# Loading image 0 once: 32 partitions first, and a gate on four 32x32 pieces of the array

## The reference

```
# layer 0
g  = relu(bn2(wg1 @ x)).mean over pixels          # 32 gates; only image 0's are used
xg = relu(tanh(wg2 @ g + bg2)) + beta             # of image 0
p  = round(xg[0:31] / sum(xg) * 96)               # assigns DCT bases to channels
y  = sum over the 7x7 cells of (cell means of x) * filt   # filt from p
x  = x * relu(bn1(w1d @ y + b1d)) + x
# layer 1
t  = relu(bn(w1 @ mean of x));  wt = w2 @ t + b2  # a 3x3 depthwise kernel per image and channel
out = depthwise conv of x with wt, masked to 4 taps, + bias
```

## Time and profile before

| what | value |
|---|---|
| time, three runs | 214.06, 214.72 (median) and 216.6 us |
| profiled execution | 213.82 us, of which the span of its instructions is 211.8 us |
| HBM | 40.51 MB read, 38.54 MB written |
| TensorE, DVE, ACT, POOL busy | 88%, 79%, 76%, 61% of the span |

### The profile page before, as it was taken

The page is one execution under the profiler, slowest core; times in us unless marked ns, Lnnn a source line. Parts: engine busy times, 40 slices in busy tenths (PEclk is TensorE's granted clock), DMA queues, the critical chain, the costliest instruction groups (busy, mean ns, idle before and its releaser), DMA issues.

```text
span 211.8 us, 4505 instructions
## 1 busy us (share of the span) xinstructions
PE 186.0 (88%) x1678; PEld 106.1 (50%) x1678; DVE 167.5 (79%) x265; ACT 161.1 (76%) x310; POOL 128.9 (61%) x120
## 2 busy tenths in 40 slices
PE   7899999799889988998899889989998989988860
PEld 3458656446445544564455546444644544554430
DVE  3338789997898689878987898798969896877780
ACT  2020027878997899789979898889888997899970
POOL 0233049999999989886997699769779110310000
PEclk9999999999999999999999999999999999999997
DMA  5999999999999999999999999999999646535777
GB/s 149 361 426 429 425 426 426 425 310 402 433 420 422 432 423 424 432 426 422 431 429 416 429 412 418 426 429 422 435 417 429 280 204 265 223 161 227 308 303 303
DMA packets 8534, 79.34 MB, mean 375 GB/s; under 512 B 1056, under 2 KB 1696, under 8 KB 2496
## 3 DMA queue, kind: packets, MB, share of 16 engines
q1 hardware_dynamic: 8352, 78.95, 90.0%
q10 hardware_dynamic: 160, 0.10, 0.2%
HBM read 40.51 MB, written 38.54 MB: 373 GB/s over the span
## 4 chain that ended last, share of the span: by engine, by line
PE 41%; ACT 30%; issue 17%; DVE 5%; DMA 2%; POOL 2%; SPq 1%; ACTq 0%; POOLq 0%
PE banks L826 16%; ACT banks L676 13%; PE banks L835 12%; ACT xout L695 9%; ACT diag L672 7%; PE banks L817 3%; PE banks L796 2%; PE banks L767 2%; DMA xout<-x 2%; PE banks L798 2%; POOL halves L378 2%; DVE stats L480 2%; PE banks L734 2%; PE banks L741 2%; DVE xout L608 1%
## 5 line engine op out<-in xcount | busy, mean ns | idle before, releaser
L826 PE MATMUL banks<-xin,diag 64*64 64x495 f32 x576 | 130.6, 584 | 15.6 <-ACT banks L676 15.6
L835 PE MATMUL banks<-xin,diag 64*64 64x385 f32 (+1 forms) x768 | 136.2, 492 | 0.0
L378 POOL TENSOR_TENSOR halves<-xin 128x1568 f32<-128x1568 f32 (+1 forms) x22 | 73.8, 3353 | 29.7 <-DMA xin<-x 21.3
L676 ACT ACTIVATE banks<-xin,wide_sb,coef 128x504 f32<-128x504 f32 x95 | 75.7, 824 | 0.7 <-DVE xout L608 0.7
L598 DVE SCALAR_TENSOR_TENSOR banks<-xin,coef,banks 128x825 f32<-128x825 f32 x48 | 51.7, 1077 | 18.8 <-ACT banks L676 18.8
L695 ACT ACTIVATE xout<-banks,wide_sb 64x392 f32<-64x392 f32 x96 | 55.9, 582 | 12.3 <-PE banks L835 10.2
L835 PEld LDWEIGHTS banks<-xin,diag 64*64 64x64 f32 x768 | 49.2, 133 | 29.2 <-issue 21.5
L826 PEld LDWEIGHTS banks<-xin,diag 64*64 64x64 f32 x576 | 39.0, 133 | 37.1 <-ACT diag L672 24.3
L608 DVE SCALAR_TENSOR_TENSOR xout<-xin,coef,banks 128x495 f32<-128x495 f32 x72 | 52.2, 724 | 4.9 <-PE banks L826 4.9
L383 POOL TENSOR_TENSOR halves<-halves 128x784 f32<-128x784 f32 x18 | 33.3, 1849 | 1.4
L672 ACT ACTIVATE diag<-wide_sb,coef 128x64 f32<-128x64 f32 x96 | 25.6, 335 | 3.2 <-DVE coef L532 2.8
(11 more groups left out here) (78 smaller groups left out, 110.1 us busy)
## 6 DMA issues: line engine op xcount, KB each, us to landing
xin<-x SPq DMA_DIRECT2D x23, 1568.0 KB, 12.3
out<-xout SPq DMA_DIRECT2D x23, 1568.0 KB, 13.1
xout<-x SPq DMA_DIRECT2D x3, 392.0 KB, 4.4
xin<-x SPq DMA_DIRECT2D x1, 1120.0 KB, 14.5
out<-xout SPq DMA_DIRECT2D x1, 924.0 KB, 4.8
wide_sb<-wide SPq DMA_DIRECT2D x1, 467.5 KB, 15.8
xin<-x SPq DMA_DIRECT2D x1, 448.0 KB, 15.1
out<-xout SPq DMA_DIRECT2D x2, 196.0 KB, 4.2
```

What stands on the lines that cost most here:

```text
L378: eng.tensor_tensor(halves[:, j % 2, first:end, :], cells[:, :, 0, :], cells[:, :, 1, :], ALU.add).then_inc(once_folded, 1)
L676: return sca.activation(acc, above_rows(k, first, end), ACT.Identity, bias=bias[:, k % PER:k % PER + 1], scale=weight(k, UP))
L826: ins = mm(to[own], diag[own, k % 2, which, :], grid(k)[own, irows, cols], start=False, stop=(which == RIGHT_UP), skip_group_check=True)
L835: ins = mm(to[other], diag[own, k % 2, which, :], grid(k)[own, irows, cols], start=(which == UP), stop=(which == LEFT), skip_group_check=True)
```

## The change

Image 0 is no longer loaded apart. The loads of tiles 0, 1 and 2 are split by partitions: partitions 0 to 31 of the three tiles come right after the gate's constants, each with a semaphore of its own; then the identity; then partitions 32 to 127 under the semaphores that the full loads had. Whoever reads a full tile of the three waits for both. `gate_one` is 32 partitions instead of 128, and DVE's three multiplications that built `gate_w` are gone. The gate reads `xin[0:32, t]` itself: in place of each product there are four, one for each quarter of the pixels, with a 32x32 weight and an output on 32 partitions of `gate_out`. TensorE waits for the identity only ahead of the first `sum_cells`.

```diff
-            sp.dma_start(gate_one[:, :], early.rearrange("(q j t) e -> q j (t e)", j=1, t=PER).broadcast_to(
-                [QUAD, GROUP, PER * E_END])).then_inc(gate_one_in, 16)
+            sp.dma_start(gate_one[:, :], early.rearrange("(q t) e -> q (t e)", t=PER)).then_inc(gate_one_in, 16)
+            def load(k, first=0, end=H, parts=slice(0, P)):
+                return sp.dma_start(xin[parts, k % IN_BUFS, PAD + first * W:PAD + end * W],
+                                    x_tiles[k // PER, k % PER][parts, first * W:end * W])
+            others = slice(QUAD, P)
+            for t in range(PER):
+                load(t, parts=slice(0, QUAD)).then_inc(image0_in[t], 16)
             sp.dma_start(wide_sb[:, 0:W_BIAS], wide[:, 0:W_BIAS]).then_inc(ident_in, 16)
-            for t in range(PER):
-                sp.dma_start(image0[:, t, :], x_image0[t]).then_inc(image0_in[t], 16)
...
-            load(0).then_inc(loaded[0], 16)
-            load(1).then_inc(loaded[1], 16)
-            load(2, 0, HEAD_PART * BLK).then_inc(part_in, 16)
-            load(2, HEAD_PART * BLK, H).then_inc(loaded[2], 16)
+            load(0, parts=others).then_inc(loaded[0], 16)
+            load(1, parts=others).then_inc(loaded[1], 16)
+            load(2, 0, HEAD_PART * BLK, others).then_inc(part_in, 16)
+            load(2, HEAD_PART * BLK, H, others).then_inc(loaded[2], 16)
...
-            dve.wait_ge(gate_one_in, 16)
-            dve.wait_ge(ident_in, 16)
-            for t in range(PER):
-                vec.tensor_tensor(gate_w[:, t, :].rearrange("p (j o) -> p j o", j=GROUP),
...
-            pe.wait_ge(gate_placed, PER)
+            pe.wait_ge(gate_one_in, 16)
             for t in range(PER):
...
-                    ins = mm(gate_out[:, part], gate_w[:, t, :], image0[:, t, part], start=(t == 0), stop=(t == PER - 1))
+                    for j in range(GROUP):
+                        pixels = slice(PAD + QUARTER * j + part.start, PAD + QUARTER * j + part.stop)
+                        ins = mm(gate_out[QUAD * j:QUAD * (j + 1), part], gate_one[:, E_END * t:E_END * t + NF],
+                                 xin[0:QUAD, t, pixels], start=(t == 0), stop=(t == PER - 1))
...
+            pe.wait_ge(ident_in, 16)
             pe.wait_ge(loaded[0], 16)
             sum_cells(0, 0, 3)
```

More of the change, by code:

```diff
@@ L72 @@
 N_END = N_TAP + TAPS * C
-W_QUARTER = 0
-W_IDENT = W_QUARTER + GROUP
+W_IDENT = 0
 W_BIAS = W_IDENT + P
@@ L117, in build @@
     out_tiles = out.rearrange("n c h w -> (n c) (h w)").rearrange("(g p t) f -> g t p f", p=P, t=PER)
-    x_image0 = x[0, :, :, :].rearrange("c h w -> c (h w)").rearrange("(q t) (j f) -> t q j f", t=PER, j=GROUP)
     with ExitStack() as ctx:
@@ L130, in build @@
         halves = sb("halves", [P, 2, DCT, BLK * W // 2])
-        gate_one = sb("gate_one", [P, PER * E_END])
-        gate_w = sb("gate_w", [P, PER, P])
+        gate_one = sb("gate_one", [QUAD, PER * E_END])
         gate_in = sb("gate_in", [P, E_HID - E_GATE2])
@@ L183, in build @@
         w_hid = wide_sb[0:C, W_HIDE:W_IMAGE]
-        quarter_of = wide_sb[:, W_QUARTER:W_IDENT]
         ident = wide_sb[:, W_IDENT:W_BIAS]
@@ L189, in build @@
         to_rows = wide_sb[0:C, W_SPREAD:W_EYE].rearrange("p (t r) -> p t r", t=PER)
-        image0 = xout[:, OUT_BUFS - 1, 0:PER * QUARTER].rearrange("p (t f) -> p t f", t=PER)
         banks = ctx.enter_context(nc.psum_tensor("banks", [P, 8, BANK], fp32))
@@ L261, in build @@
         zeroed = sem("zeroed")
-        gate_placed = sem("gate_placed")
         pad_zeroed = sem("pad_zeroed")
@@ L316, in _ @@
         def _(sp):
-            sp.dma_start(gate_one[:, :], early.rearrange("(q j t) e -> q j (t e)", j=1, t=PER).broadcast_to(
-                [QUAD, GROUP, PER * E_END])).then_inc(gate_one_in, 16)
-            sp.dma_start(wide_sb[:, 0:W_BIAS], wide[:, 0:W_BIAS]).then_inc(ident_in, 16)
-            for t in range(PER):
-                sp.dma_start(image0[:, t, :], x_image0[t]).then_inc(image0_in[t], 16)
-            def load(k, first=0, end=H):
-                return sp.dma_start(xin[:, k % IN_BUFS, PAD + first * W:PAD + end * W],
-                                    x_tiles[k // PER, k % PER][:, first * W:end * W])
+            sp.dma_start(gate_one[:, :], early.rearrange("(q t) e -> q (t e)", t=PER)).then_inc(gate_one_in, 16)
[5 more added lines that the diff above has]
+                load(t, parts=slice(0, QUAD)).then_inc(image0_in[t], 16)
+            sp.dma_start(wide_sb[:, 0:W_BIAS], wide[:, 0:W_BIAS]).then_inc(ident_in, 16)
             def store(k, first=0, end=H):
@@ L386, in _ @@
             for j in range(2):
+                pool.wait_ge(image0_in[j], 16)
                 pool.wait_ge(loaded[j], 16)
@@ L392, in _ @@
                 fold_once(j)
+            pool.wait_ge(image0_in[2], 16)
             for k in range(TILES):
@@ L542, in _ @@
             vec.tensor_scalar(count[:, :], share[:, :], ROUND, -ROUND, ALU.add, ALU.add).then_inc(counted, 1)
+            dve.wait_ge(image0_in[0], 16)
             dve.wait_ge(loaded[0], 16)
@@ L559, in _ @@
             sum_array(0).then_inc(cells_done, 1)
+            dve.wait_ge(image0_in[1], 16)
             dve.wait_ge(loaded[1], 16)
@@ L563, in _ @@
             sum_array(1).then_inc(cells_done, 1)
+            dve.wait_ge(image0_in[2], 16)
             dve.wait_ge(part_in, 16)
@@ L696, in finish_s @@
                                    bias=bias[other, k % PER:k % PER + 1]).then_inc(s_out, 1)
+            for t in range(PER):
+                act.wait_ge(image0_in[t], 16)
             act.wait_ge(folded, 4)
@@ L931, in constants @@
     w = np.zeros((P, W_END), np.float32)
-    w[:, W_QUARTER:W_IDENT] = rows[:, None] % GROUP == np.arange(GROUP)
     w[:, W_IDENT:W_BIAS] = np.eye(P)
```

## The result

The changed kernel is slower: 220.38 us median (218.75 to 226.94, 4 runs) beside 214.39 (213.65 to 216.6, 4 runs) on the same chip, ratio 1.023, 95% interval [1.015, 1.031]. The forecast was 213.3 with a range to 217.0, so it lies outside. The ratio leaves the run of 226.94 out, which was disturbed. The profiled execution took 219.46 us (217.6 of span), 5.8 us of span more than before.

What follows compares the result with a forecast made beforehand. Prediction: a rigid tile loop, waiting on no DMA, leaves when group 0's coefficients are written; gate start -0.61, gate products +0.25, tile 3 -0.76 sum to -1.1 us, from 214.4 to 213.3 us, range 212.4 to 217.0.

Steps and rivals of the forecast that it cites:

- I take full rate, since the nearest rows, the 128-partition loads, run at it: Front loads: 32-partition loads move at the 426 GB/s of full queues, 0.94 us each.
- The loads: Load queue: 1.26 MB removed, so later loads land 2.97 us earlier at 426 GB/s.
- 3.6 us early: Landing of tile 3: 2.97 us from saved bytes plus 0.62 from the queue's earlier start.
- The second rival: Front loads: partial-partition loads are slower, saved bytes bring nothing; 214.3 to 216.5 us, middle 215.4; chance 0.31.
- a rest of 0.06: Chance left for everything else, with a slower clock in the gate or a stall not named: 0.06.
- the gate starts: Gate's first product on TensorE: at 5.58 us rather than 6.19, -0.61 us.
- its products: Gate's 48 passes on 32x32 pieces, four abreast: 4.3 us instead of 4.07, +0.25 us.
- the 1.1: Departure of the tile loop, and so the end: -0.61 + 0.25 - 0.76 = -1.1 us.
- its 0.76: DVE's total, ahead of the coefficients: tile 3 lands earlier and no longer holds it up, -0.76 us.
- the gate's gain: ACT, TensorE and DVE chain behind the gate: moves with it, -0.36 us, lift coming with the gate.
- The rigid train: Tile loop: fixed length, 21.98 us per group; only its departure, when group 0's coefficients are written (30.52 us), moves.
- wait for the identity: TensorE behind the gate: the identity lands by 7 us, hidden with some 5 us to spare; uncovered, 2 us.

Runs made afterwards that it cites:

- experiment 8: The changed kernel with four full-array zero products ahead of the gate instead of one, and two ahead of each later tile: 221.03 us, ratio 1.032.
- Experiment 5: The kernel before with seven shapes of load run one after the other ahead of its work, to measure load rates: 415 GB/s for 128 partitions, 188 for 0 to 31.
- experiment 6: The kernel before, its gate and three image loads kept, with tiles 0 to 2 loaded as 32 + 96 partitions: 226.06 us, ratio 1.049.
- experiment 10: The changed kernel loading a quarter of the columns of all 128 partitions first, three quarters after; gate result not the reference's: 214.33 us, ratio 0.999.
- experiment 3: The kernel before with TensorE made to wait for the third load of image 0 ahead of tile 1 of the gate: 215.24 us, ratio 1.001.
- 2: The changed kernel with zero products ahead of gate tiles 1 and 2, run as 32x32 pieces: 221.31 us, ratio 1.028.
- 4: The kernel before, loads and gate unchanged, with six zero products from the middle of the gate on as 32x32 pieces: 217.63 us, ratio 1.014.
- experiment 11: The kernel of experiment 10 with four full zero products ahead of the gate and two ahead of each later tile: 217.69 us, ratio 1.012.

## Why the prediction was wrong

**The step that failed** is "I take full rate, since the nearest rows, the 128-partition loads, run at it". The sum for tile 3, by the steps of *The loads*: a load of 32 partitions took 2.09 us from tile to tile (8.35 - 6.26) instead of 0.94, three times 1.15 = 3.5; one of 96 took 4.79 instead of 3/4 of 3.77 = 2.83, three times 1.96 = 5.9. From 3.6 us early that makes 5.8 late. Measured, tile 4 is folded 34.57 - 29.61 = 5.0 later, and tile 3, where DVE is seen to wait for it (experiment 8), comes 31.10 - 25.78 = 5.3 later. Experiment 5 shows the rates alone, experiment 6 that the two shapes do this without the new gate, and experiment 10 that with the rate that was assumed the loss is gone. (The saved bytes are 1.30 MB rather than 1.26, with the view's KB as 1,024 bytes, as in the 0.40 MB of one load; 0.1 us, on which nothing rests.)

**The second rival had the direction and too small a price.** It took a full tile's 3.77 us as the slowest a 96-partition load could be, and so tile 3 at most 2.1 us late. No row showed that bound; the measured 4.79 adds 3 x 1.02 = 3.1 us to it. Nor does a run show this rival's half rate as such, 1.89 us for each of the first loads; they took 2.09, and the probe measured 188 GB/s beside 415. With tile 3 late by 5.0 us, total, which goes by the later of lift and tile 3, gives 214.4 + 5.0 = 219.4 in place of this rival's 216.5, and the range ended at 217.0.

**The clock was left in a rest of 0.06.** Beside the run at full rate, the changed kernel's chain is later by 0.60 us at the gate's start, then by 1.54 in the first two tiles (0.57 of it the wait for tile 1), 1.40 in the zero products, 1.32 from tile 2 to ACT, and 1.40 from ACT to the gate's second product, where TensorE was still in slow zero products (four passes in 2.98 us; 19.16 - 16.45 = 2.71, against 12.90 - 11.59 = 1.31). That is 6.26, and by_image, total and the coefficients are late by just 6.26, 6.26 and 6.25. Of these, 0.57 us are a load waited for. The row at the gate's start shows no such wait; the zero products ahead of it took 1.08 us instead of 0.82. The other 5.1 us go with the low clock, 0.50 from 10 to 18 us. Yet by experiment 8 it is hidden: without it, tile 3 holds the train to 35.84.

**What held**, measured where the loads run at the rate assumed (experiment 10): the gate starts at 5.66 (forecast 5.58); its products take 2.84 + 1.52 = 4.36 us (4.3), four pieces abreast, with their 48 weight loads (0.105 us each, PEld busy for 1.26 us) inside that time, as a load of 2.27 / 8 = 0.28 us fitted into a pass of 0.339 before; ACT's sum at 11.59 (11.4); tile 3 without a wait, total at 26.49 (26.1), coefficients at 29.96 (29.4). The departure gains 0.56 us of the 1.1, no change that can be measured: tile 3 gave its 0.76 (total at 26.49 instead of 27.25), and 0.20 of it went again behind total, while the gate's gain did not reach lift (26.11, and 26.14). The rigid train held in both kernels: 21.98 us per group. The trace of the changed kernel shows no wait for the identity, nor one at the added semaphores apart from late data.

**Left open**: what exactly lets the clock fall in the gate. A gap of 1.64 us between full products didn't (experiment 3, 1.00 after it); pieces did, with a wait only ahead of them (2, 0.50 from 10 us) and in the middle of other work (4, 0.50 from 18 us); 32 passes on pieces in a row, with no wait ahead of them or among them, didn't (10, 1.00 from 4 to 60 us). These runs give no single condition, and a run with the loads at full rate and the clock down was not made.

## What to carry over

Bytes saved are time saved only at an equal rate: a load that writes a part of the partitions can take longer than the full tile that holds it (4.79 us for 96 of them, 3.77 for all), so price both of the parts that a full load is cut into, the larger one too, or measure the shape by itself first. Where two late things end at the same place, removing either shows nothing; make the run in which the suspected common cause is gone and all else stays. And zero products that are to keep the clock up are work on the path (in experiment 11 they brought ACT's sum 4.36 us later): fill only where the engine would stand.

## What the runs showed of the hardware that I had not expected

- Partitions 32 to 127, three quarters of a tile, are written at 235 to 250 GB/s, and so take 4.79 us where all 128 take 3.77. 32 rows over every fourth partition go at 289 GB/s, into partitions 0 to 31 at 188.
- Four 32x32 pieces that share their 32 rows ran fully abreast: 32 passes of 392 columns in 2.84 us (experiment 10), where 8 full-width ones took 2.87.
- With such pieces TensorE can lose its clock: six zero products turned into pieces brought it from 1.00 to 0.50 at 18 us in the kernel before, whose time was 1.4% longer in all, though the engine was busy for 1.86 of the 2 us around the fall.
